# Rope tables of the last attention made inside the early layers and kept in memory

## The reference, cut to what matters

```python
def _L3_xattn_ref(query, key, value, position_ids, src_mask, Wq, Wk, Wv, Wo):
    q = (query @ Wq).reshape(nb, q_len, H, D).transpose(0, 2, 1, 3)   # H = 32 heads, D = 128
    k = (key @ Wk)...; v = (value @ Wv)...                            # 8 key/value heads
    cos_t, sin_t = _rope_tables(MAX_POS, D, ROPE_THETA)               # MAX_POS = 512
    cos = cos_t[position_ids][:, None]
    sin = sin_t[position_ids][:, None]
    q = q * cos + _rotate_half(q) * sin
    k = k * cos + _rotate_half(k) * sin
    scores = jnp.einsum('bhqd,bhkd->bhqk', q, k) / jnp.sqrt(jnp.float32(D))
    ...
x = x + jnp.tanh(g_xattn[2]) * _L2_xattn_ref(_layernorm(x), ctx, ...)
x = x + jnp.tanh(g_ffn[2]) * _L2_ffn_ref(_layernorm(x), ...)
x = x + jnp.tanh(g_xattn[3]) * _L3_xattn_ref(_layernorm(x), ctx, ctx, pos, mask, ...)
x = x + jnp.tanh(g_ffn[3]) * _L3_ffn_ref(_layernorm(x), ...)
```

## Time and profile before

| | |
|---|---|
| median of 3 runs | 2050.9 us (2050.52 to 2055.03) |
| the profiled execution | 2056.09 us |
| its span (first to last instruction) | 2053.9 us, mean granted TensorE clock 0.963 |
| busy share of the span | PE 91%, PEld 51%, DVE 79%, ACT 29%, POOL 32% |
| early layers | from 0 to about 1049 us |
| preparation | 1051.5 to 1104.9 us |
| last attention | from 1105.8 us |

### The profile page before, as it was taken

How to read it: one execution, slowest core, us unless ns; L and a number is a source line. 1 busy time by engine, 2 the same in 40 slices (tenths; PEclk the granted TensorE clock), 3 DMA queues, 4 the chain that set the end, 5 groups by cost and what they waited for, 6 DMA issues and landing times. The chain is left out here.

```text
span 2053.9 us, 37788 instructions
## 1 busy us (share of the span) xinstructions
PE 1871.9 (91%) x15015; PEld 1053.9 (51%) x15165; DVE 1630.7 (79%) x2908; ACT 585.7 (29%) x1347; POOL 655.3 (32%) x786
## 2 busy tenths in 40 slices
PE   8778989889889898998877999999999999999987
PEld 6434565446644456444533455555555555555543
DVE  4689776997679876797745888888888888888885
ACT  2322242223322233222333222222222222222443
POOL 3510242002420114202114544444343434343552
PEclk9899999999899998999988999999999999999997
DMA  8658204461055601463052111111111111111011
GB/s 246 186 157 229 68 2 145 124 190 57 2 165 155 195 2 42 130 195 89 2 179 77 42 32 52 52 52 48 51 42 52 52 52 52 52 32 32 16 37 52
DMA packets 142302, 176.52 MB, mean 86 GB/s; under 512 B 46769, under 2 KB 82769, under 8 KB 142001
## 3 DMA queue, kind: packets, MB, share of 16 engines
q1 hardware_dynamic: 140112, 172.88, 28.8%
q10 hardware_dynamic: 2016, 1.22, 0.3%
HBM read 131.98 MB, written 42.08 MB: 85 GB/s over the span
## 5 line engine op out<-in xcount | busy, mean ns | idle before, releaser
L1357 POOL TENSOR_TENSOR early_vare<-early_mv,w_eps 128x1 f32<-128x1 f32 x96 | 30.8, 321 | 748.3 <-DVE early_mv L1447 738.5
L2504 POOL TENSOR_TENSOR la_q<-la_straight,la_rot 128x512 f32<-128x512 f32 x128 | 163.0, 1273 | 160.3 <-DVE la_rot L2588 160.3
L441 PE MATMUL la_ps<-w_xTl,w_wqh 128*128 128x512 bf16 x512 | 196.8, 384 | 5.1 <-DVE la_rot L2588 3.8
L441 PE MATMUL la_ps<-w_wol,la_oTh 128*128 128x512 bf16 x512 | 194.0, 379 | 6.3
L440 PE MATMUL la_ps<-w_xTh,w_wqh 128*128 128x512 bf16 x505 | 194.9, 386 | 3.9 <-DVE la_rot L2588 3.8
L442 PE MATMUL la_ps<-w_xTh,w_wql 128*128 128x512 bf16 x510 | 195.4, 383 | 0.0
L442 PE MATMUL la_ps<-w_woh,la_oTl 128*128 128x512 bf16 x512 | 194.0, 379 | 0.0
L2517 POOL TENSOR_TENSOR la_p<-la_s,la_rec 128x256 f32<-128x256 f32 x128 | 89.6, 700 | 272.6 <-DVE la_rec L2609 269.9
L2434 ACT ACTIVATE la_oTh<-la_ps 128x256 bf16<-128x256 f32 x256 | 84.0, 380 | 295.0 <-PE la_ps L2317 295.0
L1607 DVE TENSOR_TENSOR early_products<-early_pR,early_vR 128x4096 f32<-128x4096 f32 x32 | 140.1, 4421 | 16.5 <-DMA early_pR<-scr_p 16.5
L440 PE MATMUL la_ps<-w_woh,la_oTh 128*128 128x512 bf16 x391 | 148.2, 379 | 0.0
(11 more groups left out here) (360 smaller groups left out, 4623.5 us busy)
## 6 DMA issues: line engine op xcount, KB each, us to landing
early_vR<-scr_v SPq DMA_DIRECT2D x128, 257.0 KB, 5.4
early_wkv<-wkv SPq DMA_DIRECT2D x32, 512.0 KB, 4.2
la_v<-v SPq DMA_DIRECT2D x64, 256.0 KB, 4.0
k<-early_ctxt SPq DMA_DIRECT2D x32, 256.0 KB, 3.9
v<-early_ctxt SPq DMA_DIRECT2D x64, 128.0 KB, 2.5
scr_p<-early_weights SPq DMA_DIRECT2D x16, 512.0 KB, 5.1
early_pR<-scr_p SPq DMA_DIRECT2D x32, 256.0 KB, 3.7
w_raw_q<-in_Wq SPq DMA_DIRECT2D x8, 1024.0 KB, 7.4
```

What stands on the lines that cost most here:

```text
L441: pe.matmul(out, lh[c], rl[c], start=False, stop=False)
L2504: rope_sum.send(pool.tensor_tensor(dst, straight[:, slot, :], rot[:, slot, :], ALU.add))
```

## The change

The table product moves out of the preparation into each turn of the early layers, in two halves of 256 tokens (`rope(turn, half)`), which take the place of the idle products before the last `turn_weights` and before "gturn". DVE makes the one-hot matrix of a turn's 512 tokens in `osb` after the experts' scaling of layer 1's feed-forward. ACT copies each half twice: to `rope_out` (cos and sin), and sin with its sign turned to `rope_minus`. SP loads the turn's positions (256 KB) ahead of the next turn's x, the table (256 KB) into `hs`, and writes both results to memory (`rope3`, 384 KB a turn). The preparation then only loads cos and sin in four transfers of 512 KB. It loses `hot`, `rope`, `half_rope` and `double`, and both groups of idle products; x is the first thing loaded, PSUM banks 0 to 7 serve the transposes of even and odd turns, and on ACT high_q stands ahead of normalise(2) and high ahead of high_q. The last attention loses `double` and its waits.

```diff
@@ early_layers
+        if j == QUAD - 1:
+            plan.append((("rope", 0), 3))
...
-    plan += [(("gate2",), 4), (("route2",), 5), (("gturn",), 6)]
+    plan += [(("gate2",), 4), (("route2",), 5), (("rope", 1), 7), (("gturn",), 6)]
...
+        pos, table, one_hot = sb("pos", [P, D]), hs, osb
+        rope_out = hsT[:, :, :].rearrange("p j n -> p (j n)")
+        rope_minus = rh[:, :, :].rearrange("p j n -> p (j n)")[:, 0:D]
...
+            def load_positions(turn):
+                banks.wait_filled(sp, turn, "out1", QUAD - 1)
+                pos_in.send(sp.dma_start(pos[:, :], io["pos3"][bass.ts(turn, D)].partition_broadcast(P)))
+            def load_table(turn):
+                banks.wait_filled(sp, turn, "hturn", 1, QUAD - 1)
+                table_in.send(sp.dma_start(table[:, :, :], io["rope"].rearrange("(c p) n -> p c n", p=P)))
+            def keep_rope(turn):
+                banks.wait_drained(sp, turn, "rope", 1)
+                rope_kept.send(sp.dma_start(io["rope3"][turn, 0:P, :], rope_out))
+                minus_kept.send(sp.dma_start(io["rope3"][turn, P:P + 64, :], rope_minus[64:P, :]))
             def store(turn):
+                load_table(turn)
+                keep_rope(turn)
                 for j in range(QUAD):
                     x_done.wait(sp, turn, j)
...
+            def rope(turn, half):
+                if half == 0:
+                    hot_ready.wait(pe, turn, 0)
+                    table_in.wait(pe, turn, 0)
+                banks.wait_free(pe, turn, "rope", half)
+                cols = slice(half * (D // 2), (half + 1) * (D // 2))
+                for c in range(C):
+                    last = pe.matmul(banks.bank("rope", half)[:, 0:D // 2], table[:, c, :], one_hot[:, c, cols],
+                                     start=(c == 0), stop=(c == C - 1))
+                banks.fill(last, "rope", half)
...
-                idle_products(4 if more else 9, turn, "gturn")
+                rope(turn, 1)
...
+            def rope_copy(turn, half):
+                cols = slice(half * (D // 2), (half + 1) * (D // 2))
+                banks.wait_filled(act, turn, "rope", half)
+                act.activation(rope_out[:, cols], banks.bank("rope", half)[:, 0:D // 2], ACT.Copy)
+                banks.drain(act.activation(rope_minus[64:P, cols], banks.bank("rope", half)[64:P, 0:D // 2], ACT.Copy,
+                                           scale=-1.0), "rope", half)
...
                 expo_ready.send(act.activation(e2[:, :, :], e2[:, :, :], ACT.Exp))
+                rope_copy(turn, 1)
                 banks.wait_filled(act, turn, "gturn")
...
                 lora(1, R1)
+                pos_in.wait(dve, turn, 0)
...
+                for c in range(C):
+                    last = dve.tensor_scalar(one_hot[:, c, :], pos[:, :], row[:, c:c + 1], None, ALU.is_equal)
+                hot_ready.send(last)
@@ prepare_last
-            plan.append((("turn", t, j), j))
-        plan.append((("rope", t), 4 + t % 2))
+            plan.append((("turn", t, j), QUAD * (t % 2) + j))
...
-            pos_loaded.send(sp.dma_start(pos[:, :], io["pos3"].partition_broadcast(P)))
-            table_loaded.send(sp.dma_start(table[:, :, :], io["rope"].rearrange("(c p) n -> p c n", p=P)))
+            def load_rope(tile, half, row):
+                rope_loaded.send(sp.dma_start(
+                    w[tile][64 * half:64 * half + 64, :].rearrange("p (t n) -> p t n", t=TURNS),
+                    io["rope3"][:, row:row + 64, :].rearrange("t p n -> p t n")))
...
@@ last_attention, on POOL
-            rope_sum.wait(pool, 0, len(FIRST) - 1)
-            double(2)
-            double(3)
             clear_stale(pool, w)
```

More of the change, by code:

```diff
@@ L1146, in route_exp @@
                 n = nr + LORA
+                if f == 0 and turn > 0:
+                    rope_kept.wait(act, turn - 1, 0)
+                    minus_kept.wait(act, turn - 1, 0)
                 for j in range(QUAD):
@@ L1874, in _ @@
             rstd_of(2)
-            double(0)
             rstd_of(3)
@@ L1947, in _ @@
             normalise(0)
-            half_rope(0)
             normalise(1)
             high(0)
-            half_rope(1)
-            normalise(2)
             act.wait_ge(q_loaded.sem, 16)
@@ L1981, in statistics @@
                 dve.sem_inc(stats_ready.sem, 1)
-            def hot(t):
-                if t >= 2:
-                    banks.wait_filled(dve, 0, "rope", t - 2)
-                for c in range(C):
-                    last = dve.tensor_scalar(one_hot[:, t % 2, c, :], pos[:, tokens(t)], row[:, c:c + 1], None, ALU.is_equal)
-                hot_ready.send(last)
             def low(t):
@@ L2583, in rotate @@
                     src = banks.bank(*step)
-                if turn == 0 and n >= 2:
-                    doubled.wait(dve, 0, 2 * (n - 2) + 1)
                 dve.tensor_tensor(straight[:, slot, :], src, w["cos"][:, tokens(n)], ALU.mult)
```

86 lines of the change are left out of this document (25 added, 61 removed).

## The result

| | before | after |
|---|---|---|
| median | 2051.66 us (2050.52 to 2055.03, 5 runs) | **2041.3 us** (2036.2 to 2051.68, 5 runs) |
| profiled execution, its span, granted clock | 2056.09, 2053.9, 0.963 | 2037.34, 2035.6, 0.966 |

The ratio after to before is 0.9947, with a 95% interval of 0.9926 to 0.9969: about 11 us faster, and between 6.4 and 15.2. A later repeat of the same kernel gave 0.9944 (0.9925 to 0.9963). The forecast was 2041.6 us, a gain of 9.3 us.

What follows compares the result with a forecast made beforehand. PE's idle products held the barrier before the last attention, and a DVE, POOL, ACT chain set the preparation. 9.7 + 0.55 + 0 - 0.9 = 9.35, rounded 9.3: 2050.9 - 9.3 = 2041.6 us, range 2036.5 to 2048.5.

Steps and rivals of the forecast that it cites:

- The preparation, 9.7: Stage before the last attention: 9.7 us gained, first load to first matmul 44.6 us instead of 54.3.
- the idle products: End of the preparation: PE's 16 idle products no longer hold the barrier, 2.4 us gained.
- the order of the loads: Start of the preparation: x goes ahead of positions and table, 3.3 us gained.
- The opening, clock term 0: Last attention's opening: PE's clock effects taken as 0, between a gain of 2.1 and a loss of 1.75 us.
- the term of q0: First matmuls of the last attention: PE starts at half clock, q0 1.4 us later, at worst 2.55.
- q3's clock: PE's restart for q3 in the opening: 2.7 us shorter if at full clock after some 2.1 us idle.
- POOL's doubling, 0.55: Last attention's opening: four POOL doubling instructions leave, gaining only PE's 0.55 us wait for la_p, not 5.0.
- The early layers, +0.9: Table work before gturn delays ACT's rT copy 0.3 us in turns 2 to 4: 0.9 us lost.
- (d): Rival: q3 fast, POOL's clears no bound, longer products before gturn keep the clock up; 13 us gained, 2037.9; chance 0.09.
- (a): Rival: PE starts cold and stays so through the last attention's opening; 5.0 us gained, 2045.9; chance 0.20.
- (b): Rival: the table work shows in the early layers, some 8 us; 1.3 us gained, 2049.6; chance 0.14.
- (c): Rival: cos and sin transfers hold the preparation if below 89 GB/s; at 50 GB/s 2060 us; chance 0.04.

Runs made afterwards that it cites:

- e3: Kernel before with preparation and last attention of after, cos and sin read from rows of x instead of the tables: 2039.87 us, ratio 0.9943 to before.
- e2: Kernel before with the early layers of after, tables stored but not read: 2049.78 us, ratio 0.9990 to before.
- e4: Kernel before with eight idle products instead of four before gturn and instead of six before each turn's last turn_weights, no table work: 2050.13 us, ratio 0.9991.
- e1: Kernel before without the 16 idle products at the preparation's end: 2050.39 us, ratio 0.9993 to before.
- e11: Kernel after with the old loads of positions and table put back ahead of x, into unread tiles: 2043.87 us, ratio 0.9947 to before.
- e6: Kernel after with four POOL instructions of the doubling's length back in the opening, writing an unread tile: 2038.44 us, ratio 0.9937 to before.
- e8: Kernel after with loads, ACT, DVE and POOL's clears reordered in the preparation, tables on 128 partitions, eight idle products at its end: 2042.09 us, ratio 0.9955.
- e9: Kernel after with the preparation's loads, ACT, DVE and POOL's clears reordered, tables loaded as in after, no end idle products: 2030.44 us, ratio 0.9886 to before.
- e12: Kernel after, unchanged, run once more for its spread: 2043.94 us, ratio 0.9944 to before.
- e7: Kernel after with cos and sin loaded in eight transfers of 128 partitions, cos reading the same 64 rows twice: 2043.21 us, ratio 0.9959 to before.
- e10: As e9, with sin loaded in four transfers of 128 partitions and cos as in after: 2031.20 us, ratio 0.9893 to before.
- e5: Kernel after with ten idle products back at the end of the preparation: 2039.94 us, ratio 0.9950 to before.

## Why the prediction was right, step by step

**The preparation, 9.7: right.** Measured were 9.5, and 9.75 in e3. Its steps held within tenths: normalise(0) 10.9 behind the first load (10.6 forecast), the first matmul 44.8 (44.6). POOL's clears held the first factor as written, by 0.5 instead of 0.9. Some of the agreement is luck: with the same order of instructions the preparation took 54.35 in before, 54.11 in e2 and 53.53 in e4, as x(0) came later or sooner, and against the mean of the three the gain is 9.2. Of its parts the idle products were 2.3 (e1; forecast 2.4) and the order of the loads 2.5 (e11; forecast 3.3, sized by the position of x in before and not by the two loads that went). The rest is 4.7 by subtraction. The rows place 4.3 of it between normalise(0) and the last low, where half_rope and high_q stood on ACT's chain; no run put these two back alone.

**The opening, clock term 0: inside its range, for q0 near the worst, for q3 near the best.** The forecast took 0 between a gain of 2.1 and a loss of 1.75. Measured on the way to q3's rotation: q0 2.37 later (11 of its 12 matmuls wholly slow, where the forecast counted 6.5 and 1.4 us and allowed up to 2.55), 0.78 back from the first rotation instruction of the keys (0.69 instead of 1.47; forecast 0.8, though the second still took 1.66), and 2.54 back at q3 (forecast 2.7 if its clock stayed up): 0.95 gained. So the term of q0 was set 1.0 too small, and taking 0 for q3's clock left out a gain that came. That q3's clock stays up is no luck of one trace: after, e1, e3, e6, e8, e9 and e12, which start cold, have the rotation of q3 at 15.2 (e7, e10 and e11, where PE rose sooner within q0, at 14.1 to 15.1), and before and e4, with a warm start, at 16.1. Only e2 had both, a warm start and a fast q3, at 13.6, after the same 3.00 of idle that slowed e4. So what a wait of 3.0 does to PE differs from run to run, and waits of 1.8 to 2.23 left it fast in all of these.

**POOL's doubling, 0.55: about right, for one clock.** Of the 2.0 us of the opening, 0.95 come up to q3's rotation and 1.06 behind it: the wait of 0.55 is gone, and two matmuls fewer are slow behind the restart (0.43). e1, with the doubling in place and the same opening up to the restart, shows a wait of 0.50, e4 of 0.51. e6 shows none, with eleven slow matmuls behind the restart. The forecast took the wait of one trace for the price; it is the difference of two times, la_p's and PE's own, and the second moves with the clock. Of the 5 us that POOL's own chain shows, only what makes la_p later than PE was ever at stake.

**The early layers, +0.9: right in place, and too small to be seen in the time.** In the trace of after, 0.3 show in each of the first three turns, whose ends are all of the shorter kind, and 0.47 in the last one; where a turn's end is the longer kind, as in e2's second turn, nothing shows. The forecast had 0.3 in turns 2 to 4 and nothing in turn 1. Together these are 1.1 in e2's trace and 1.4 in after's, while e2's ratio (0.9976 to 1.0004) has 0.8 us slower at its end. So how much of what the turns' ends show reaches the end of the kernel stays open. Wrong was a detail: the 1.6 by which DVE's result was later in the first turn is not that turn's, it falls on any. Rival (d)'s thought, that longer products keep the clock up there, has no support: e4 has the longer products and the usual length.

**Rivals.** (a) was half right, as PE did start cold and q0 lost 2.37 of the 2.55; but q3 was not slow as before, and the opening came out 2.0 shorter instead of longer. (b) fell with e2. (c) did not occur, at 206 GB/s where 89 would have begun to hurt; e7 and e8 show that it is real in kind: 49 GB/s on a part of the load cost 5.7 us in e7 and some 13 us of barrier in e8. (d) had q3 right and POOL's clears and the early layers wrong.

**The sum** of 9.3 stands against some 11 by the ratios. The clock in the opening accounts for about one of the difference; the rest is inside the interval of 6.4 to 15.2.

## What to carry to other kernels

Write the stages as distances between marks (first load, first matmul, a fixed product) and compare those over several traces. First load to first matmul repeated to 0.2 us with after's preparation (44.60 to 44.82 in five traces), while the time of one execution moved by up to 15. Not every distance is so steady: the opening took 32.3 to 36.2 with the same instructions and the early layers 1046 to 1053, so ask first how far a mark moves by itself.

When a chain passes through several engines, ask on each what stands ahead of the link without being part of it; a new order of the loads, of ACT, DVE and POOL's clears, with all statistics first, was worth as much again as the whole change (e9).

Before warming PE for a stretch, look at the next wait in it: a warm start that only lengthens that wait can be given back there, as in e5. And a wait that a trace shows is the difference of two times: before it is taken for a price, look in other traces how far the later one of the two moves.

## What the runs showed of the hardware

- Loads lost speed in two ways: those of 64 partitions ran at 197 to 215 GB/s with all DMA engines busy (stretches of 2 us in e9), against 385 with 128; and those of 256 KB whose source has a slowest dimension of 2 at 49 GB/s (e7). The queue behind such a load waits too: the mask of e7 made DVE wait 5.63.
- One unchanged kernel spread from 2036.2 to 2051.7 us in five runs, with mean granted clocks of 0.969 and 0.957; the same early layers took 1045.96 to 1053.38 over ten traces.
- How long PE stays at the half clock behind equal waits differs from run to run. Behind 3.76 to 3.78 of idle in the opening 5 matmuls were slow in after and e12, 6 in e3, e8 and e9, 7 in before, e1 and e4, 11 in e2, e5, e6 and e10. Behind 3.59 in e7 and e11 none was. In the openings of after the second la_p follows: at 34.7 to 34.9 behind the first matmul with 5 or 6 slow ones, at 36.0 to 36.2 with 11, and at 32.3 to 32.6 in e7 and e11, where q0's rotation also came 0.8 to 1.1 sooner.
- POOL's 109 semaphore clears at the start of after's preparation took 8.0 us, 0.07 each, and the first factor started right behind them, 0.5 later than the statistics allowed.
